# Routed rows in 256-row tiles among attention slots, and three score units for a causal group

## The chip, the cores and the metric

The kernel runs on one core of a Trainium2 chip. The metric is the device time of one execution in microseconds (us); lower is better. Five engines work side by side and meet only at semaphores: TensorE (PE; its weight loads are listed as PEld), VectorE (DVE), ScalarE (ACT), GpSimd (POOL) and SyncE (SP). In this kernel SyncE issues every DMA before the change.

## The reference, cut to what matters

```python
# x: (8, 256, 128), ctx_1024: (8, 512, 128)
x = x + tanh(g_xattn[0]) * L0_xattn(layernorm(x), ctx)      # 16 heads of 8, keys from ctx
x = x + tanh(g_ffn[0])   * L0_ffn(layernorm(x))             # one expert of eight for each row
x = x + tanh(g_xattn[1]) * L1_xattn(layernorm(x), ctx)      # self attention, cross attention, FFN, norms between
x = x + tanh(g_ffn[1])   * L1_ffn(layernorm(x))             # causal attention with rotary, then two experts of four

def L0_ffn(x):                                              # E = 8, D = 128, H = 512
    top1 = argmax(xf @ gate_w.T + gate_b)
    for e in range(8):
        y = relu(xf @ w1[e].T + b1[e]) @ w2[e].T + b2[e]
        out = out + where(top1 == e, y, 0)
```

Everything is float32. The inputs are drawn from a seed; which rows go to which expert is known only when the kernel runs.

## The kernel before

**Batches.** There are four attentions (att0: cross, att1: self, att2: cross, att3: causal) and eight batches of 256 rows in each. One number n from 0 to 31 counts them; `body(n)` is one batch of one attention. A body is a row of slots: 16 in att0 and att2 (512 keys, one head a slot), 8 in att1 and att3 (256 keys, two heads a slot). Its items are put at 16 positions, so that a slot of att1 or att3 holds two positions.

**What a slot does.** `E` multiplies keys by queries into a half of `e_ps` (1024 columns of PSUM), ScalarE takes the exponential into the ring `prob`, and `AV` multiplies by the values into `av_ps`. The softmax's row maxima are needed before `E`: the step `S` computes the same scores earlier, into one of the two halves of `s_ps` in units of 512 columns (two units for each head pair or head), and VectorE reduces each unit to maxima (`nmax`). `S` runs 2*gs + 1 slots ahead of `E`, where gs is the slots of a group of four heads. When a group is whole, GpSimd splits the maxima into bfloat16 parts (`maxsplit`), TensorE turns them (`maxT`, into `misc`), ScalarE copies them to `mrow`, and a DMA brings them into row 72 and on of `Qst`, from where the next `E` reads them.

**misc.** The PSUM buffer `misc` (512 columns) is shared by all small matmuls: projections, turns, gates. Each use first waits until the one before it was copied out (`misc_drained`).

**Order.** `all_steps()` writes one list, `STEPS`; every engine, SyncE's queue too, goes through it in this order and does its part of each step. Nothing is reordered later. Batch n's slots carry the projections of batch n + 2, the loads of n + 1 to n + 3 and the output steps of n - 1.

**First mixture.** `RUNS = [(0, B), (B, N)]` cuts the list after att0. Between the two runs `moe0_steps` does the mixture in four blocks of 512 rows. For each of eight experts and four pieces of the hidden 512, `m0.h` is a 128x512 matmul with weights `w1_0` into `e_ps` (L1496), ScalarE applies the relu into `prob` (L974), VectorE multiplies by the row's mask for that expert (L1207; the mask is spread by L1491 into `s_ps`), and `m0.down` adds the output matmul to `av_ps` (L1503). All rows go through all experts. Weights for all eight (4 MB) are loaded into `wbig` during att0. The step also writes the transposed rows that att1 loads as `inT`.

**Causal attention.** In att3 an `S` unit holds one head: two matmuls of 256 columns (L1369) and three mask matmuls of 128 (L1372, L1373, L1375), four units for a group of four heads.

## Time and profile before

| | us |
|---|---|
| median of 3 runs | 1477.69 |
| lowest, highest | 1476.61, 1484.08 |
| the profiled execution, its time | 1473.35 |
| its span, first to last instruction | 1471.6 |
| TensorE busy | 1279.9 |
| VectorE busy | 882.1 |
| ScalarE busy | 693.7 |
| GpSimd busy | 305.0 |

The mean granted clock of TensorE is 0.933 of full. All stretches below are given in us from the span's start. Matmuls are pipelined, so that a stretch in which TensorE is busy is not one in which it starts a matmul as early as it could; the distance between two starts tells that. A float32 matmul stands in the trace as two records, one for each pass.

### The profile page before, as it was taken

The numbers are of one execution on the slowest core, as the hardware profiler recorded it, in microseconds if no ns is written. First come the engines' busy times: TensorE is split into PE (matmuls) and PEld (weight loads), VectorE is DVE, ScalarE is ACT, GpSimd is POOL, SyncE is SP. The second block draws the span as 40 slices with busy tenths as digits, with TensorE's granted clock in tenths as the row PEclk, the third lists the DMA queues.
The fourth block names the chain that finished last, engine by engine and source line by source line (L and its number), as shares of the span: only waits on it lengthen the run. The fifth ranks groups of instructions, "written<-read, shape, count | busy, mean of one in ns | idle before, by whom it ended". The sixth has DMA issues, their size and how long they took to land.

```text
span 1471.6 us, 25336 instructions
## 1 busy us (share of the span) xinstructions
PE 1279.9 (87%) x8424; PEld 673.2 (46%) x8424; DVE 882.1 (60%) x1922; ACT 693.7 (47%) x1064; POOL 305.0 (21%) x896
## 2 busy tenths in 40 slices
PE   3999989979999998878879997887888788879998
PEld 1444444534444443445435444444555566634343
DVE  2777677833444444477658777868675866633333
ACT  1466566633333332566637665644533334423333
POOL 3223222100001000333422331312232322100000
PEclk9999899989999999799969999999989989869999
DMA  7554444210001300465644453533333434220110
GB/s 183 164 155 142 131 146 129 70 48 8 15 21 38 106 21 1 139 173 158 181 141 150 125 169 97 156 97 98 101 102 105 132 89 129 63 55 15 29 29 14
DMA packets 163175, 144.40 MB, mean 98 GB/s; under 512 B 11739, under 2 KB 136931, under 8 KB 163043
## 3 DMA queue, kind: packets, MB, share of 16 engines
q1 hardware_dynamic: 163046, 142.79, 33.6%
q8 instruction: 68, 1.11, 0.3%
q14 instruction: 61, 0.50, 0.1%
HBM read 79.05 MB, written 62.91 MB: 96 GB/s over the span
## 4 chain that ended last, share of the span: by engine, by line
issue 60%; POOLq 20%; PE 15%; DVE 3%; DMA 1%; DVEq 1%; ACT 1%; POOL 0%; SPq 0%; PEldq 0%; ACTq 0%
POOLq L865 4%; POOLq L838 4%; PE e_ps L1566 3%; PE av_ps L1577 3%; PE e_ps L1567 3%; POOLq L835 2%; POOLq L840 2%; POOLq L875 2%; POOLq L873 2%; POOLq L877 1%; PE misc L1558 1%; DVE nmax L1092 1%; PE s_ps L1369 1%; PE av_ps L1415 1%; PE misc L1349 1%
## 5 line engine op out<-in xcount | busy, mean ns | idle before, releaser
L924 ACT ACTIVATE prob<-e_ps 128x1024 f32<-128x1024 f32 (+1 forms) x384 | 378.1, 988 | 244.1 <-PE e_ps L1397 176.2
L1088 DVE TENSOR_REDUCE nmax<-s_ps 128x1 f32<-128x512 f32 x512 | 332.7, 686 | 115.5 <-PE s_ps L1363 113.6
L1397 PE MATMUL e_ps<-Qst,Kst 75*128 75x256 bf16 x1408 | 241.3, 285 | 19.6 <-DMA Qst<-mrow 12.6
L1363 PE MATMUL s_ps<-Kst,Qst 72*128 72x512 bf16 x512 | 206.3, 407 | 44.0 <-DVE nmax L1088 33.1
L1092 DVE TENSOR_REDUCE nmax<-s_ps 128x2 f32<-128x512 f32 x256 | 171.2, 687 | 106.2 <-PE s_ps L1369 56.4
L1415 PE MATMUL av_ps<-prob,Vx 128*32 128x256 f32 (+1 forms) x3072 | 220.6, 406 | 0.8 <-ACT OT L929 0.8
L1397 PEld LDWEIGHTS e_ps<-Qst,Kst 75*128 75x128 bf16 x1408 | 137.7, 101 | 87.6 <-issue 22.3
L1207 DVE TENSOR_TENSOR prob<-prob,s_ps 128x512 f32<-128x512 f32 x128 | 87.8, 687 | 147.4 <-ACT prob L974 146.7
L974 ACT ACTIVATE prob<-e_ps,b 128x512 f32<-128x512 f32 x128 | 87.9, 687 | 147.4 <-PE e_ps L1496 146.7
L1369 PE MATMUL s_ps<-Kst,Qst 72*128 72x256 bf16 x512 | 119.4, 294 | 22.7 <-DVE nmax L1092 21.9
L1496 PE MATMUL e_ps<-FB,wbig 128*128 128x512 f32 x256 | 137.2, 627 | 0.0
L1503 PE MATMUL av_ps<-prob,wbig 128*128 128x512 f32 x256 | 128.1, 592 | 0.0
L1415 PEld LDWEIGHTS av_ps<-prob,Vx 128*32 128x32 f32 x3072 | 92.0, 116 | 72.6 <-issue 39.7
L1363 PEld LDWEIGHTS s_ps<-Kst,Qst 72*128 72x128 bf16 x512 | 50.3, 99 | 149.3 <-DVE nmax L1088 110.4
L929 ACT ACTIVATE OT<-av_ps 128x256 f32<-128x256 f32 x128 | 49.1, 384 | 95.5 <-PE av_ps L1415 95.4
L872 POOL TENSOR_TENSOR mparts<-nmax,zeros 128x8 bf16<-128x8 f32 x128 | 25.6, 200 | 310.4 <-DVE nmax L1088 166.2
L1313 DVE TENSOR_TENSOR prob<-prob 128x512 f32<-128x512 f32 x48 | 33.2, 693 | 88.6 <-ACT prob L1012 88.1
L1503 PEld LDWEIGHTS av_ps<-prob,wbig 128*128 128x128 f32 x256 | 48.6, 190 | 61.2 <-issue 53.1
L1369 PEld LDWEIGHTS s_ps<-Kst,Qst 72*128 72x128 bf16 x512 | 48.3, 103 | 61.9 <-DVE nmax L1092 29.7
L959 ACT ACTIVATE mrow<-misc 12x256 bf16<-12x256 bf16 x128 | 46.4, 363 | 55.9 <-PE misc L1444 55.6
L1496 PEld LDWEIGHTS e_ps<-FB,wbig 128*128 128x128 f32 x256 | 47.1, 196 | 53.3 <-issue 52.3
L1011 ACT ACTIVATE prob<-e_ps 128x512 f32<-128x512 f32 x48 | 28.7, 597 | 84.4 <-PE e_ps L1567 84.3
(179 smaller groups left out, 1624.1 us busy)
## 6 DMA issues: line engine op xcount, KB each, us to landing
q_parts<-qp SPq DMA_DIRECT2D x96, 192.0 KB, 2.4
k_parts<-kp SPq DMA_DIRECT2D x48, 384.0 KB, 3.4
Qst<-q_parts SPq DMA_DIRECT2D x128, 144.0 KB
Kst<-k_parts SPq DMA_DIRECT2D x64, 288.0 KB
k_parts<-kp SPq DMA_DIRECT2D x48, 192.0 KB, 2.4
Kst<-k_parts SPq DMA_DIRECT2D x64, 144.0 KB
ctxT<-in_ctxT SPq DMA_DIRECT2D x16, 256.0 KB, 4.6
wbig<-in_w SPq DMA_DIRECT2D x16, 256.0 KB, 4.8
```

What stands on the lines that cost most here:

```text
L838: po.drain()
L924: act.activation(dst, src, ACT.Exp).then_inc(e_drained, 1)
L974: act.activation(hid[:, c % 8, :], hid_ps[:, c % 4, :], ACT.Relu, bias=b1_0[:, e, t:t + 1]) \
L1088: ve.tensor_reduce(nmax[:, g, u, h % GH:h % GH + 1], s_ps[:, u, :], AX.X, ALU.max, negate=True).then_inc(s_drained, 1)
L1092: ve.tensor_reduce(nmax[:, g, :, h % GH:h % GH + 1], s_ps[:, u, :].rearrange("p (t k) -> p t k", t=QT), AX.X, ALU.max, negate=True).then_i ...
L1207: ve.tensor_tensor(gated[:, c % 8, :], hid[:, c % 8, :], s_ps[:, mk % 2, :], ALU.mult) \
L1363: last = pe.matmul(s_ps[:, u, :], Qst[0:ROWS, par, s, u * P:u * P + P], Ks[0:ROWS, par, s, :], start=True, stop=True)
L1369: last = pe.matmul(o, Qst[0:ROWS, par, h, t * P:t * P + P], Ks[0:ROWS, par, h, 0:SQ], start=True, stop=not a.rope)
L1397: last = pe.matmul(o, Ks[0:KROWS, par, h, t * P:t * P + P], Qst[0:KROWS, par, h, :], start=True, stop=not a.rope)
L1415: last = pe.matmul(av_ps[VW * hh:VW * hh + VW, SQ - w:SQ], Vx[:, par, t, h, :], prob[:, place, off * SQ:off * SQ + w], start=(t == 0), sto ...
L1496: pe.matmul(hid_ps[:, c % 4, :], w1_0[:, e, t * P:t * P + P], x, start=True, stop=True) \
L1503: pe.matmul(av_ps[:, :], w2_0[:, e, t, :], gated[:, c % 8, :], start=False, stop=end) \
```

## The change

It does three things.

**Rows by expert.** Eight batches make two halves (`HALF` = 4). As each batch of att0 ends, its rows are normed into `zg`, gated (`m0.gate`), the expert is chosen (`m0.choose`), and `m0.rank` counts by matmul how many earlier rows of the half chose the same expert. When the half is complete, `m0.plan` makes two tables: `ypos`, the place of each row in a list sorted by expert, where each expert starts at a multiple of 256, and `widx`, the weight rows of each of the NT = 11 tiles. GpSimd then issues indexed DMAs: `m0.scatter` writes rows of `zg` to their places in `xs_rows` (zeroed at the start from `blank`), `m0.wload` reads a tile's weights and biases (128 rows of 1032 numbers) into a ring of four. For each tile follow `m0.xT` (turn), `m0.h` (4 matmuls of 256 columns), `m0.down` (4 more), `m0.back` (turn) and a store to `ys_rows`.

**Among the slots.** `RUNS` is one run. `moe0_items` puts the steps at positions: for the first half tiles in bodies 5 and 6, for the second in 9 and 10, a tile every 4/3 positions. att1's batches no longer load `inT`. They load `x1`, gather their rows of `ys_rows` by `ypos` (GpSimd), add (`xstat`), norm (`xapply`), turn (`xT`) and store x2 and z (`xstore`).

**Causal groups.** In att3 a group of four heads is three `S` units: one with the first 128 rows of all four heads against the first 128 keys, two with the other 128 rows of two heads each. The third mask is gone.

```diff
-RUNS = [(0, B), (B, N)]
+RUNS = [(0, N)]
...
+def moe0_items():
+    it = {}
+    def put(n, p, *steps):
+        it.setdefault((n + p // 16, p % 16), []).extend(steps)
+    for b in range(B):
+        if b % HALF < HALF - 1:
+            for p, kind in ((3, "m0.gate"), (6, "m0.choose"), (9, "m0.rank")):
+                put(b + 2, p, (kind, b, None))
+    for g in range(B // HALF):
+        last = HALF * g + HALF - 1
+        n = last + 1
+        for p, kind in ((12, "m0.gate"), (13, "m0.choose"), (14, "m0.rank")):
+            put(n, p, (kind, last, None))
+        for k in range(3):
+            put(n, 15 + k, ("m0.plan", g, k))
+        n += 1
+        put(n, 0, ("m0.wload", g, 0), ("m0.wload", g, 1))
+        for j in range(GT):
+            put(n, 2 + j // 4, ("m0.scatter", g, j))
+        put(n, 4, ("m0.wload", g, 2), ("m0.wload", g, 3), ("m0.xload", g, 0), ("m0.xload", g, 1))
+        for k in range(NT):
+            p = 5 + 4 * k // 3
+            put(n, p, ("m0.xT", g, k))
+            if k + 2 < NT:
+                put(n, p, ("m0.xload", g, k + 2))
+            put(n, p + 1, ("m0.h", g, k))
+            put(n, p + 2, ("m0.down", g, k))
+            if k + WRING < NT:
+                put(n, p + 2, ("m0.wload", g, k + WRING))
+            put(n, p + 3, ("m0.back", g, k))
+        m = B + HALF * g
+        put(m - 2, 9, ("loadx", m, None))
+        put(m - 2, 11, ("xstat", m, None), ("loadx", m + 1, None))
+        put(m - 2, 13, ("xapply", m, None), ("xT", m, None))
+        put(m - 2, 14, ("q", m, None), ("qsplit", m, None), ("xstore", m, None))
+        put(m - 2, 15, ("k", m, None), ("ksplit", m, 0), ("xstat", m + 1, None))
+        put(m - 1, 0, ("qstore", m, None))
+        put(m - 1, 2, ("kstore", m, None))
+    return it
...
-    if n + 2 < hi:
-        if n + 2 < B:
+    if n + 2 < hi and not opens_half(n + 2):
+        if n + 2 < 2 * B:
             put(0, ("xapply", n + 2, None))
             put(1, ("xT", n + 2, None))
+            if n + 2 >= B:
+                put(2, ("xstore", n + 2, None))
...
-def moe0_steps(plan):
...
+                elif kind == "m0.xload":
+                    if arg == 0:
+                        sp.wait_ge(m0_sent, 16 * GT * (n + 1))
+                    if m0_tile(n, arg):
+                        prev = (n, arg - 2) if arg >= 2 else (n - 1, NT - 1 if (NT - 1) % 2 == arg else NT - 2)
+                        sp.wait_ge(misc_filled, MISC[("m0.xT",) + prev] + 1)
+                    src = xs_rows[n][arg * TILE:(arg + 1) * TILE, :].rearrange("(t p) d -> p t d", p=P)
+                    sp.dma_start(xs_in[:, arg % 2, :, :], src).then_inc(m0_xin[arg % 2], 16)
+                elif kind == "m0.back":
+                    sp.wait_ge(misc_drained, MISC[(kind, n, arg)] + 1)
+                    dst = ys_rows[n][arg * TILE:(arg + 1) * TILE, :].rearrange("(t p) d -> p t d", p=P)
...
+                elif kind == "xstore":
+                    sp.wait_ge(x_normed, n + 1)
+                    sp.dma_start(batch_rows("x2", b), xr[:, par, :, :]).then_inc(x_stored[par], 16)
+                    sp.dma_start(batch_rows("z", b), xn[:, :, :]).then_inc(z_stored, 16)
...
+            for g in range(B // HALF):
+                blank = dram["blank"].unsqueeze(0).to_broadcast([NT, TILE, D])
+                sp.dma_start(xs_rows[g].rearrange("(n r) d -> n r d", r=TILE), blank).then_inc(blank_stored, 16)
...
+                elif kind == "m0.wload":
                     po.drain()
-                    po.wait_ge(f_stats, f_stat("m0", n, 0))
-                    rsqrt(LF, BT, False).then_inc(f_rstd, 1)
+                    po.wait_ge(m0_planned, 2 * n + 1)
+                    if arg >= WRING:
+                        po.wait_ge(misc_drained, MISC[("m0.down", n, arg - WRING)] + 1)
+                    elif n:
+                        po.wait_ge(misc_drained, MISC[("m0.down", n - 1, NT - 1)] + 1)
+                    index = bass.IndirectOffsetOnAxis(ap=widx[:, n, arg:arg + 1], axis=0)
+                    po.indirect_dma_start(out=w_0[:, arg % WRING, :], out_offset=None, in_=dram["w_0"], in_offset=index) \
+                        .then_inc(m0_win[arg % WRING], 16)
+                elif kind == "m0.scatter":
+                    po.drain()
+                    po.wait_ge(m0_planned, 2 * n + 2)
+                    po.wait_ge(blank_stored, 16 * B // HALF)
+                    index = bass.IndirectOffsetOnAxis(ap=ypos[:, n, arg:arg + 1], axis=0)
+                    po.indirect_dma_start(out=xs_rows[n], out_offset=index, in_=zg[:, arg, :], in_offset=None) \
+                        .then_inc(m0_sent, 16)
+                elif kind == "loadx" and n >= B:
+                    par, g = n % 2, (n - B) // HALF
+                    po.drain()
+                    po.wait_ge(m0_ystored[0], 16 * Y_EVEN * (g + 1))
+                    po.wait_ge(m0_ystored[1], 16 * Y_ODD * (g + 1))
+                    po.wait_ge(x_stats, n - 1)
+                    for t in range(QT):
+                        j = QT * (n % HALF) + t
+                        index = bass.IndirectOffsetOnAxis(ap=ypos[:, g, j:j + 1], axis=0)
+                        po.indirect_dma_start(out=yg[:, par, t, :], out_offset=None, in_=ys_rows[g], in_offset=index) \
+                            .then_inc(y_back[par], 16)
                 elif kind == "f.stat":
...
+                elif kind == "m0.xT":
+                    act.wait_ge(misc_filled, MISC[st] + 1)
+                    if arg >= 2:
+                        act.wait_ge(e_filled, SLOT[("m0.h", n, arg - 2)] + 1)
+                    act.activation(xs_T[:, arg % 2, :], misc[:, 0:TILE], ACT.Copy).then_inc(misc_drained, 1)
                 elif kind == "m0.h":
...
+                    for t in range(H0 // P):
+                        b1 = w_0[:, arg % WRING, 2 * H0 + t:2 * H0 + t + 1]
+                        last = act.activation(m0_hid[:, arg % 2, t * TILE:(t + 1) * TILE],
+                                              e_ps[:, c % 2, t * TILE:(t + 1) * TILE], ACT.Relu, bias=b1)
...
+                    elif a.rope:
+                        k = s % a.gs * a.units(0) + u
+                        dst = nmax[:, g, 1, 2 * k - 2:2 * k] if k else nmax[:, g, 0, :]
+                        ve.tensor_reduce(dst, s_ps[:, c % 2, :].rearrange("p (h k) -> p h k", h=2 if k else GH), AX.X,
+                                         ALU.max, negate=True).then_inc(s_drained, 1)
...
                 elif kind == "xstat":
                     ve.wait_ge(x_loaded[par], 16 * (n // 2 + 1))
+                    if n >= B:
+                        ve.wait_ge(y_back[par], 16 * QT * ((n - B) // 2 + 1))
+                        ve.scalar_tensor_tensor(out=xr[:, par, :, :], in0=yg[:, par, :, :], scalar=gate_of("moe0"),
+                                                in1=xr[:, par, :, :], op0=ALU.mult, op1=ALU.add)
...
-                        apply_norm(LA, dst, newres[:, par, :, :], QT).then_inc(norm_ready, 1)
+                        if n >= HALF:
+                            ve.wait_ge(m0_sent, 16 * GT * (n // HALF))
+                        j = QT * (n % HALF)
+                        apply_norm(LA, zg[:, j:j + QT, :], newres[:, par, :, :], QT).then_inc(norm_ready, 1)
                     else:
...
+                    elif a.rope:
+                        g, k = s // a.gs, s % a.gs * a.units(0) + u
+                        heads, t, w = (range(2 * k - 2, 2 * k), 1, SQ) if k else (range(GH), 0, P)
+                        for x, h in enumerate(heads):
+                            o = s_ps[:, c % 2, x * w:x * w + w]
+                            h += GH * g
+                            pe.matmul(o, Qst[0:ROWS, par, h, t * P:t * P + P], Ks[0:ROWS, par, h, 0:w], start=True,
+                                      stop=False)
+                            last = pe.matmul(o[:, w - P:w], identb[:, :], maskb[:, 0, :], start=False, stop=True)
...
+                elif kind == "m0.rank":
+                    if n == 0:
+                        pe.wait_ge(below_made, 1)
                     pe.wait_ge(m0_chosen, n + 1)
-                    for t in range(BT):
-                        last = pe.transpose(misc[0:E0, :].bitcast(BF16)[:, t * P:t * P + P], ohb[:, t, :], identb[:, :])
+                    total = misc[:, QT * E0:QT * E0 + E0]
+                    pe.matmul(misc[:, 0:E0], below[:, :], ohb[:, 0, :], start=True, stop=True)
+                    pe.matmul(misc[:, E0:2 * E0], below[:, :], ohb[:, 1, :], start=True, stop=False)
+                    pe.matmul(misc[:, E0:2 * E0], onesb[:, :], ohb[:, 0, :], start=False, stop=True)
+                    pe.matmul(total, onesb[:, :], ohb[:, 0, :], start=True, stop=False)
+                    pe.matmul(total, onesb[:, :], ohb[:, 1, :], start=False, stop=True).then_inc(misc_filled, 1)
+                elif kind == "m0.xT":
+                    pe.wait_ge(m0_xin[arg % 2], 16 * (m0_tile(n, arg) + 1))
+                    turn(misc, lambda t: xs_in[:, arg % 2, t, :], QT).then_inc(misc_filled, 1)
+                elif kind == "m0.h":
+                    c = SLOT[st]
+                    pe.wait_ge(m0_win[arg % WRING], 16 * (w_uses(n, arg) + 1))
+                    pe.wait_ge(misc_drained, MISC[("m0.xT", n, arg)] + 1)
+                    pe.wait_ge(e_drained, c - 1)
+                    for t in range(H0 // P):
+                        last = pe.matmul(e_ps[:, c % 2, t * TILE:(t + 1) * TILE], w_0[:, arg % WRING, t * P:t * P + P],
+                                         xs_T[:, arg % 2, :], start=True, stop=True)
+                    last.then_inc(e_filled, 1)
+                elif kind == "m0.down":
+                    pe.wait_ge(e_drained, SLOT[("m0.h", n, arg)] + 1)
+                    for t in range(H0 // P):
+                        w2 = w_0[:, arg % WRING, H0 + t * P:H0 + t * P + P]
+                        last = pe.matmul(misc[:, 0:TILE], w2, m0_hid[:, arg % 2, t * TILE:(t + 1) * TILE],
+                                         start=t == 0, stop=t == H0 // P - 1)
                     last.then_inc(misc_filled, 1)
-                elif kind == "m0.mask0":
-                    pe.wait_ge(misc_drained, MISC[("m0.spread", n, None)] + 1)
```

On TensorE, in body 5. In the names `FB` with `ident` is a turn of a tile (`m0.xT` or `m0.back`), `FB` with `wbig` is `m0.h`, `m_hid` with `wbig` is `m0.down`. Before, from the values of batch 6 on:

```order
L1438 MATMUL misc<-wts,ctxT 128x128 x4
L1363 MATMUL s_ps<-Kst,Qst 128x512
L1397 MATMUL e_ps<-Qst,Kst 128x256 x4
L1363 MATMUL s_ps<-Kst,Qst 128x512
L1455 MATMUL misc<-wts,aT 128x128 x2
L1415 MATMUL av_ps<-prob,Vx 32x256 x8
```

and the same place after:

```order
L1560 MATMUL misc<-wts,ctxT 128x128 x4
L1470 MATMUL misc<-ident,FB 128x128 x2
L1613 MATMUL e_ps<-FB,wbig 128x256 x4
L1470 MATMUL misc<-ident,FB 128x128 x2
L1484 MATMUL s_ps<-Kst,Qst 128x512
L1521 MATMUL e_ps<-Qst,Kst 128x256 x4
L1484 MATMUL s_ps<-Kst,Qst 128x512
L1577 MATMUL misc<-wts,aT 128x128 x2
L1620 MATMUL misc<-m_hid,wbig 128x256 x4
L1613 MATMUL e_ps<-FB,wbig 128x256 x4
L1470 MATMUL misc<-ident,FB 128x128 x2
L1537 MATMUL av_ps<-prob,Vx 32x256 x8
```

In one slot seven groups for the tiles now stand where none stood, four of them on `misc`.

On GpSimd, in body 5. Before:

```order
L837 TENSOR_TENSOR qk<-qk,qp 128x256
L839 CAST qp<-qk 128x256
L841 TENSOR_TENSOR qp<-qk,qp 128x256
L872 TENSOR_TENSOR mparts<-nmax,zeros 128x2x4
L874 TENSOR_TENSOR mres<-nmax,mparts 128x8
```

and after (`wbig<-in_w,widx` is `m0.wload`, `xs_rows<-wbig,ypos` is `m0.scatter`):

```order
L941 DMA wbig<-in_w,widx 128x1032 x2
L883 TENSOR_TENSOR qk<-qk,qp 128x256
L885 CAST qp<-qk 128x256
L887 TENSOR_TENSOR qp<-qk,qp 128x256
L948 DMA xs_rows<-wbig,ypos 2816x128 x4
L918 TENSOR_TENSOR mparts<-nmax,zeros 128x2x4
L920 TENSOR_TENSOR mres<-nmax,mparts 128x8
L922 CAST mparts<-mres 128x2x4
L924 TENSOR_TENSOR mparts<-mres,mparts 128x2x4
L948 DMA xs_rows<-wbig,ypos 2816x128 x4
```

Ten indexed DMAs now stand around the first `maxsplit` of the body.

On SyncE, at the start of the program, after the change:

```order
L703 DMA gw<-in_gw 128x4
L868 DMA xs_rows<-in_blank 11x2x16384 x2
L806 DMA q_parts<-qp 128x3x256 x3
L811 DMA k_parts<-kp 128x3x512 x3
L821 DMA Qst<-q_parts 72x1024
```

The two copies of zeros stand between the last constant and the first batch's Q.

## Rows read from the trace of the kernel before

**Rows 1.** The page: busy us, share of the span, instructions of each engine.
```profile
PE 1279.9 (87%) x8424; PEld 673.2 (46%) x8424; DVE 882.1 (60%) x1922; ACT 693.7 (47%) x1064; POOL 305.0 (21%) x896
```

**Rows 2.** Stages: length; busy us of PE, PEld, DVE, ACT, POOL; PE clock; DMA share; GB/s.
```profile
48.00:303.00 255.00, 232.00 (x1980) 124.66 (x1979) 188.83 (x384) 164.98 (x230) 66.67 (x200) 0.96 0.45 129
303.00:594.80 291.80, 272.03 (x746) 118.55 (x745) 119.11 (x242) 100.51 (x154) 14.45 (x31) 0.94 0.12 35
594.80:773.50 178.70, 150.07 (x1210) 83.33 (x1209) 117.40 (x245) 103.00 (x167) 62.83 (x196) 0.86 0.53 157
1073.00:1295.00 222.00, 187.24 (x1918) 134.75 (x1915) 150.92 (x399) 84.22 (x151) 63.56 (x198) 0.89 0.35 103
```

**Rows 3.** Exp alone (L924): length, ACT busy (count) by stretch; then two starts.
```profile
47.00:303.00 256.00, 128.39 (x126) 0.96 0.45 130
...
301.46 3.00 ACT L924 ACTIVATE prob<-e_ps 128x1024 f32<-128x1024 f32 x3
...
594.76 1.02 ACT L924 ACTIVATE prob<-e_ps 128x1024 f32<-128x1024 f32 x1 [4.21 <-PE e_ps L1397]
```

**Rows 4.** Groups, 303:594.8, PE: shapes, count | busy us, mean ns | idle before, releasers.
```profile
L1369 PE MATMUL s_ps<-Kst,Qst 72*128 72x256 bf16 x22 | 5.3, 347 | 4.8 <-DVE nmax L1092 4.5 <-PE av_ps L1503 0.3
L1349 PE MATMUL misc<-ident,OT 128*128 128x128 f32 x24 | 4.8, 336 | 1.1 <-DVE att_o L1139 0.7 <-DVE lg L1188 0.4
...
L1415 PE MATMUL av_ps<-prob,Vx 128*32 128x256 f32 x48 | 3.0, 382 | 0.8 <-ACT OT L929 0.8
L1349 PE MATMUL misc<-ident,FB 128*128 128x128 f32 x16 | 2.4, 272 | 0.0
L1430 PE MATMUL misc<-inT,wts 128*128 128x256 f32 x8 | 2.4, 379 | 0.0
L1397 PE MATMUL e_ps<-Qst,Kst 75*128 75x256 bf16 x12 | 2.3, 321 | 3.6 <-DMA Qst<-mrow 3.6
...
L1455 PE MATMUL misc<-wts,aT 128*128 128x128 f32 x4 | 1.2, 460 | 0.5 <-ACT aT L963 0.5
```

**Rows 5.** Timeline, PE, inside the mixture: start, us, line, operation, count.
```profile
571.46 1.02 PE L1496 MATMUL e_ps<-FB,wbig 128*128 128x512 f32 x2
572.32 1.02 PE L1503 MATMUL av_ps<-prob,wbig 128*128 128x512 f32 x2
```

**Rows 6.** Timeline, PE, ahead of the mixture, with [idle before <-releaser].
```profile
313.62 1.12 PE L1349 MATMUL misc<-ident,OT 128*128 128x128 f32 x4 [0.72 <-DVE att_o L1139]
...
316.62 1.22 PE L1455 MATMUL misc<-wts,aT 128*128 128x128 f32 x4 [0.47 <-ACT aT L963]
```

**Rows 7.** Waits (us in total, times, longest), 48:303; then those of PE, 594:773.
```profile
PEld s_ps L1363 <- DVE nmax L1088: 38.0, 72, 1.9
...
PE e_ps L1397 <- DMA Qst<-mrow: 11.5, 11, 3.6
```

**Rows 8.** Groups, ACT, whole span: copy of 256 columns with a bias.
```profile
L938 ACT ACTIVATE qk<-misc,qbias 128x256 f32<-128x256 f32 x24 | 11.3, 470 | 8.5 <-PE misc L1430 8.5
```

**Rows 9.** Timeline of SyncE's queue at the start; then a stretch as in rows 2.
```profile
6.91 5.39 SPq L658 DMA_DIRECT2D ropes<-in_ropes  x1
...
18.89 1.47 SPq L767 DMA_DIRECT2D q_parts<-qp  x3
...
29.68 0.31 SPq L785 DMA_DIRECT2D Kst<-k_parts  x1
...
25.00:50.00 25.00, 16.52 (x36) 3.98 (x36) 13.03 (x24) 3.85 (x7) 7.67 (x19) 1.00 0.68 197
```

**Rows 10.** Timeline, PE and DVE, one S unit of the fourth attention.
```profile
1181.42 0.27 PE L1369 MATMUL s_ps<-Kst,Qst 72*128 72x256 bf16 x1
1181.53 0.22 PE L1372 MATMUL s_ps<-maskb,identb 128*128 128x128 bf16 x1
1181.59 0.22 PE L1373 MATMUL s_ps<-maskb,identb 128*128 128x128 bf16 x1
...
1182.01 0.69 DVE L1092 TENSOR_REDUCE nmax<-s_ps 128x2 f32<-128x512 f32 x1
```

535 lines of the change are left out of this document (250 added, 285 removed).

## The prediction

> **What bounds the kernel now.** I read the page's totals first, then the busy times by stage, then in each stage which wait ends last.
>
> TensorE is busy for 87% of the span and VectorE for 60% [rows 1]; the others come behind. By stage [rows 2] TensorE is at 91% in the first attention, at 93% between 303 and 594.8 us, where the first mixture lies, at 84% in the second attention and in the fourth. The mixture is TensorE alone: half the way through one hidden and one output matmul of 512 columns leave in 0.86 us each, two passes of 0.43 us, with no gap [rows 5], and all four blocks pay for all eight experts. The last Exp of the eighth batch starts at 303.4 (the third of three from 301.46), the first of the ninth at 594.76 [rows 3]: 291.4 us without a score. That is a fifth of the span, and the change aims at it.
>
> The attention stages are not bound by TensorE's columns. A slot of the first attention takes 256/126 = 2.03 us [rows 3], and the waits there are for the row maxima that VectorE takes, 38.0 us of them [rows 7]. In the second attention TensorE also waits for the maxima's way through GpSimd and DMA, 11.5 us for the DMA that brings them to `Qst` [rows 7].
>
> **The change part by part.** The sum is made against the profiled span.
>
> *The dense mixture goes.* Of the 291.4 us, attention work stays and only moves: in the window's groups [rows 4] S 5.3, OT turns 1.6 (8 of the 24; 4.8/3), AV 3.0, projections 2.4, E 2.3, and five more kinds, the largest of them the projection by the output weights with 1.2, for which I count 3.7 in all. That is 18.3 us, so **−273**.
>
> *Twenty-two tiles come.* Four batches are 1024 rows; tiles of 256 rows with eight experts make 4 + 7 = 11 in a run, and there are two runs. A tile has 8 matmuls of 256 columns in float32. A pass of 512 columns is 0.43 us, two passes a matmul, so 256 columns cost 0.43: 3.4 us. Four turns of 128 columns are 0.15 each (2.4 us for 16 [rows 4]), 0.6. Five groups each end in a pipeline that the next cannot overlap; I give 0.1 us to each: 4.5 us of TensorE. Besides, a tile uses the one PSUM buffer `misc` three times, and each use waits until the last one was drained. Such a round trip is 0.72 us over VectorE and 0.47 over ScalarE in the row before the mixture [rows 6]. The order puts `m0.back`, `m0.down`, `m0.h`, `m0.xT` side by side, so I count two of the three as unhidden: 1.2. ScalarE has six copies of 256 columns in a tile, at most 0.47 us each [rows 8], 2.8 us against 5.7: it keeps up. The hidden units lie behind about one slot of attention before `m0.down` wants them, so I take this as hidden. 5.7 us a tile, **+125**. Ends: 4.5 (all round trips covered; slots of 2.03 us hold room for that) and 8.5 (ScalarE's 2.8 us stands in the path of each tile), so +99 to +187.
>
> *Routing per batch.* Gate and rank are seven small matmuls with two uses of `misc`, 0.72 + 0.47 us of round trips [rows 6], and a dozen short VectorE operations in front of the maxima, which delay TensorE by their length at most. The gate work of before was inside the stage taken away. I take 2 us a batch between 1 (the round trips alone) and 3.5: **+16** (8 to 28).
>
> *Opening of a run.* GpSimd now issues two weight gathers and eight scatters before the first `m0.xload`, and SyncE waits there for all scatters. Behind it in SyncE's queue stand the max rows of the running batch and its Q and K. No row shows an indexed DMA. The nearest rows are SyncE's issues, from 0.31 us for a K load to 5.39 for the rope tables [rows 9]. I take 1.0 us, nearer the short end, since the long one stood at a full queue. Ten issues are 10 us, where the batch has four positions: 8 us in the first attention, 5 in the second, and then three slots until the max rows are wanted. I take 3 + 9 = **+12** (3 to 40).
>
> *Start.* Two copies of 1.44 MB of zeros stand in SyncE's queue ahead of the first Q and K stores. At full share the queues there move 197/0.68 = 290 GB/s [rows 9]: 10 us from about 18.9, with Q and K (1.8 MB, 6 us) behind it, where K is wanted at 29.68. 18.9 + 10 + 6 = 34.9, **+5** (0 to 14). On this the Trainium skill says more: by its page "DMA: Bandwidth & Descriptors", section "Why a DMA increments its semaphore by 16 and not by 1", a copy is spread on the largest number of engines up to 16 that divides its slowest dimension, here 11 tiles, hence 11 engines. By that the zeros would take 14.5 us and the term would be +9.5. No row here shows such a copy; it stays inside the bounds.
>
> *Second attention.* It no longer loads its input but makes it: statistics, norm and turn for each batch, with two gathers on GpSimd, 2.0 us by the price above, in a stage where GpSimd stands between maxima and E [rows 7], and one more `misc` round trip of 0.47. 8 batches at 2.5 us, **+20** (8, nearly all hidden, to 40, issues of 2 us and more), and at the two places where a half opens the gather has two positions to land, **+5** (2 to 10). The loads and stores of the old block form go; they were off the path.
>
> *Fourth attention.* Three S units per group for four. A unit of before leaves in 0.40 us (two of 256 columns at 0.11, three masks at 0.06) and its maximum takes 0.69 [rows 10]. A group now has 0.48 + 2×0.34 = 1.16 us for 1.6, and one maximum less. Over 32 groups that is 14 us of TensorE and 22 of VectorE. At 84% TensorE and with both engines relieved I take **−16** (−5 to −22).
>
> Sum: −273 + 125 + 16 + 12 + 5 + 20 + 5 − 16 = −106. 1471.6 − 106 = 1365.6 us of span. The profiled run took 1473.35, and the median of the three is 1477.69, 6.1 above the span: **1372 us**.
>
> One rule of the Trainium skill speaks against the change. "SBUF — State Buffer", section "Who interferes with whom", says that a DMA issued by GpSimd cannot have its descriptors written while VectorE runs a copy, cast or tensor_scalar in its two-port mode. Rows show such VectorE work only as short pairs of norm instructions beside long maxima, so by it each issue might wait some tenths of a microsecond, 10 us in all for 54 issues; no trace here has such a DMA yet.
>
> **The rivals.**
> *Round trips hidden.* The slots' own room (2.03 us against a TensorE content near 1.7) and VectorE's freed time cover them: tiles at 4.5 us, openings 5, routing 10, second attention 12. −273 + 99 + 10 + 5 + 5 + 12 + 3 − 18 = −157: 1321. For it: waits for maxima fall away where tiles stretch a slot. Against: each misc use has one buffer.
> *Latency in the path.* Tiles at 8.5 us because ScalarE's relus sit between h, down and the next misc drain, as the queue order allows: 22 × 2.8 = +62, 1434. For it: `m0.xT` is drained behind the relus of `m0.h`.
> *Slower.* Indexed DMAs are dear on GpSimd. Each extra microsecond per issue costs 20 us at the openings (ten issues, twice) and some 10 at the 16 gathers in the second attention, which are partly covered: 30 in all; the 22 weight gathers stay behind four tiles of lead. From 1.0 + 106/30 = 4.5 us per issue the gain is gone; at 5 us the kernel takes 1493. For it: the 5.39 us row. Against: that one waited for a full queue.
> *Not doing what it says.* The tiles come, but serialised behind SyncE's waits so that attention does not run beside them. Then the work adds as in the sum, since TensorE is the bound either way; it falls in with the second rival.
>
> **How the numbers follow.** Forecast, a gain of 75 to 135 us: 0.63. Hidden round trips: 0.19. Latency in the path or issues near 3 us: 0.12. Issues of 4.5 us or more: 0.05 (0.01 of it no change). No change by other mishaps: 0.01. The range for 8 in 10 is 1318 to 1434: it cuts half of the hidden case, and beyond the latency case. About 0.5% is what a measurement of this kernel can tell from no change: faster by more 0.94, within 0.02, slower 0.04.
>
> **What would show it.** Weight matmuls of 256 columns 0.43 us apart; about 6 us of TensorE time per tile, and idle time before `misc` matmuls ended by ScalarE and VectorE; at both openings a hole before an E, ended by the max rows' DMA, near 3 and 9 us; the first Exp about 5 us later than before; bodies 13 to 15 a little longer than now; the fourth attention at about 206 us for 222. A weight gather that ends idle time of TensorE would make the tile term wrong; a GpSimd issue above 3 us would make the opening wrong.

## The result, and the profile after

The changed kernel takes 1490.87 us (median; 1480.98 to 1501.68), the kernel before, timed beside it, 1474.61 us. The ratio is 1.013, with a 95% interval of 1.010 to 1.016. The forecast was 1372 us. A gain of 7% was expected and a loss of 1.3% came.

The profiled execution took 1501.18 us, with a span of 1499.4; that is 10 us above its own median, where the profiled execution of before lay near its own. The traces therefore differ by more (27.8 us of span) than the medians (16.3). The page's totals, in the columns of [rows 1]:

```profile
PE 1161.3 (77%) x8192; PEld 658.8 (44%) x8192; DVE 797.7 (53%) x1863; ACT 654.2 (44%) x1069; POOL 363.1 (24%) x958
```

TensorE has 119 us less to do than in [rows 1], and the kernel is not faster: it waits. The waits of TensorE from 230 to 600 us, a stretch that holds both openings (us in total, times, longest):

```profile
PE misc L1470 <- DMA FB<-xs_rows: 43.1, 2, 29.0
PE misc L1566 <- POOL mparts L924: 23.1, 3, 15.1
```

Stretches cut at the bodies' first Exps, in the columns of [rows 2]: length; busy us of PE, PEld, DVE, ACT, POOL; clock; DMA share; GB/s. The second and the fourth hold the tiles of the two halves.

```profile
55.00:242.00 187.00, 162.62 (x1299) 86.59 (x1297) 133.69 (x307) 108.60 (x154) 50.88 (x144) 0.94 0.39 118
242.00:425.00 183.00, 124.31 (x754) 77.37 (x753) 62.31 (x143) 67.70 (x128) 39.27 (x75) 0.82 0.28 87
...
493.50:657.40 163.90, 95.12 (x538) 66.51 (x536) 39.81 (x99) 51.54 (x110) 37.15 (x71) 0.78 0.29 88
657.40:801.40 144.00, 106.54 (x775) 58.44 (x776) 82.25 (x181) 67.53 (x109) 49.73 (x139) 0.79 0.49 148
801.40:1108.00 306.60, 263.27 (x2122) 140.92 (x2120) 222.60 (x487) 172.62 (x242) 80.97 (x228) 0.94 0.41 122
```

In the two stretches with tiles TensorE is busy for 68% and 58%, where it was at 93% in the dense mixture [rows 2].

Two starts of the Exp, as in [rows 3]. The first comes 6.9 us later than before (47.94 then):

```profile
54.87 1.02 ACT L994 ACTIVATE prob<-e_ps 128x1024 f32<-128x1024 f32 x1 [5.80 <-PE e_ps L1521]
```

```profile
801.39 1.94 ACT L994 ACTIVATE prob<-e_ps 128x1024 f32<-128x1024 f32 x2 [0.38 <-PE e_ps L1521]
```

Now the first opening on GpSimd, part of body 5 (start, us, line, operation, idle before). L941 is a weight gather, L948 a scatter, L918 to L924 the split of a group of maxima:

```profile
245.99 1.18 POOL L941 DMA_INDIRECT wbig<-in_w,widx  x1 [3.67 <-DVE widx L1327]
252.18 0.95 POOL L941 DMA_INDIRECT wbig<-in_w,widx  x1 [5.01 <-issue]
256.41 0.67 POOL L883 TENSOR_TENSOR qk<-qk,qp 128x256 f32<-128x256 f32 x1 [3.28 <-issue]
...
259.32 1.03 POOL L948 DMA_INDIRECT xs_rows<-wbig,ypos  x1 [0.88 <-issue]
262.49 0.99 POOL L948 DMA_INDIRECT xs_rows<-wbig,ypos  x1 [2.13 <-issue]
265.59 0.97 POOL L948 DMA_INDIRECT xs_rows<-wbig,ypos  x1 [2.11 <-issue]
...
282.46 0.96 POOL L948 DMA_INDIRECT xs_rows<-wbig,ypos  x1 [2.10 <-issue]
```

The DMA itself is recorded with 1.0 us, the price that the forecast took. But the next instruction comes 3.1 us after a scatter's start and 6.2 and 4.2 us after a weight gather's. Between them stands `po.drain()`. How long a scatter takes from its issue to its landing, in us, from the DMA issues between 259 and 284 us:

```profile
xs_rows<-wbig,ypos POOLq DMA_INDIRECT x8, 2.2
```

The drains stand in the trace as records of their own. Those ahead of the scatters, with their shortest, median and longest time in ns:

```profile
L944 POOLq DRAIN  x16: 301/2537/2607, 257.7 to 531.2; - x16
```

In the whole trace 46 drains stand behind an indexed DMA that had not landed when they began. They last 2.5 to 6.8 us, and every one of them ends 0.07 to 0.13 us after the last of these DMAs has landed, whether that takes 2.2 us from the issue (a scatter) or 6.5 (the slowest weight gather). The other 902 drains last 0.29 us in the median and 1.10 at most, as the 894 in the kernel before do. So the length of such a drain is the landing of the DMA, and from its end to the start of the next scatter pass another 0.8 us.

SyncE's queue at the same time. It stands at `m0.xload` (L715) until all scatters have landed, and the maxima's row (L828) is behind it:

```profile
247.90 0.36 SPq L824 DMA_DIRECT2D Kst<-k_parts  x1
284.70 0.89 SPq L715 DMA_DIRECT2D FB<-xs_rows  x2
285.64 0.73 SPq L828 DMA_DIRECT2D Qst<-mrow  x1
```

And TensorE, which waits first for the split of the maxima and then for the first tile's rows:

```profile
257.05 0.38 PE L1484 MATMUL s_ps<-Kst,Qst 72*128 72x512 bf16 x1
272.52 0.37 PE L1566 MATMUL misc<-identb,mparts 128*12 128x128 bf16 x2 [15.09 <-POOL mparts L924]
286.92 0.66 PE L1470 MATMUL misc<-ident,FB 128*128 128x128 f32 x2 [14.02 <-DMA FB<-xs_rows]
```

In the second half, in att1, the two holes are 7.8 and 29.0 us.

**Where the 134 us between forecast and trace lie.** The first Exps of the 32 bodies cut the span. Each term of the sum against what the cuts show, in us of span; the last column is an experiment's kernel, below.

| term | forecast | changed kernel | self_wait |
|---|---|---|---|
| dense mixture goes (body 7 with the mixture: 312.4, then 35.6 and 34.2) | -273 | -277 | -278 |
| 22 tiles | +125 | +143 | +132 |
| openings, both halves | +12 | +74 | +33 |
| routing, second attention, landing (16 + 20 + 5) | +41 | +81 | +62 |
| start | +5 | +7 | -2 |
| third attention | 0 | +7 | +10 |
| fourth attention and what follows | -16 | -7 | -10 |
| sum | -106 | +28 | -53 |

The tile row is made from the slots with tile steps: 101.6 us in the bodies 5 and 6 where the same slots took 28.3 before, and 86.8 for 17.3 in the bodies 9 and 10. An opening is the slots from a body's start to its first tile: body 5's slots 0 to 5 took 48.9 us for 13.9, body 9's slots 0 to 2 took 47.1 for 8.1.

The drains, which self_wait takes out, and the zeros, which it moves, account for some 80 of the 134 us (a span of 1419.1 for 1499.4). The other 53 are still there in its column, 21 of them at the openings and 21 in the row of routing and second attention.

### The profile page after: what moved, and what is told of

It reads as the page before. It is cut to its first block, busy times and chain, and to the rows that moved or that the text cites. A ratio compares the mean times of both kernels' runs of the same rounds, so it can differ in the third digit from the quotient of the medians.

```text
span 1499.4 us, 25002 instructions
## 1 busy us (share of the span) xinstructions
PE 1161.3 (77%) x8192; PEld 658.8 (44%) x8192; DVE 797.7 (53%) x1863; ACT 654.2 (44%) x1069; POOL 363.1 (24%) x958
## 4 chain that ended last, share of the span: by engine, by line
issue 54%; POOLq 22%; PE 17%; DVE 2%; ACT 2%; DMA 1%; POOL 1%; DVEq 1%; SPq 0%; ACTq 0%; PEldq 0%
POOLq L911 5%; POOLq L884 4%; PE e_ps L1678 3%; PE av_ps L1689 3%; PE e_ps L1679 3%; PE misc L1620 2%; POOLq L881 2%; POOLq L886 2%; PE e_ps L1613 2%; POOLq L919 2%; POOLq L921 2%; POOLq L923 2%; PE misc L1470 1%; POOLq L944 1%; PE misc L1670 1%
## 5 line engine op out<-in xcount | busy, mean ns | idle before, releaser
L1537 PE MATMUL av_ps<-prob,Vx 128*32 128x256 f32 (+1 forms) x3072 | 234.2, 427 | 0.0
L1176 DVE TENSOR_REDUCE nmax<-s_ps 128x2 f32<-128x512 f32 x128 | 86.4, 687 | 164.8 <-PE s_ps L1498 164.3
L1484 PEld LDWEIGHTS s_ps<-Kst,Qst 72*128 72x128 bf16 x512 | 51.4, 101 | 148.4 <-DVE nmax L1167 99.4
L918 POOL TENSOR_TENSOR mparts<-nmax,zeros 128x8 bf16<-128x8 f32 x128 | 26.3, 205 | 357.5 <-DVE nmax L1167 198.9
L1172 DVE TENSOR_REDUCE nmax<-s_ps 128x2 f32<-128x512 f32 (+1 forms) x96 | 65.9, 687 | 57.7 <-PE s_ps L1494 57.3
L1566 PE MATMUL misc<-identb,mparts 128*12 128x128 bf16 x256 | 37.6, 232 | 63.7 <-POOL mparts L924 35.6
L1470 PE MATMUL misc<-ident,FB 128*128 128x128 f32 x136 | 27.3, 298 | 75.1 <-DMA FB<-xs_rows 43.1
L1620 PE MATMUL misc<-m_hid,wbig 128*128 128x256 f32 x176 | 54.2, 461 | 14.8 <-DVE FB L1343 10.4
L1498 PE MATMUL s_ps<-Kst,Qst 72*128 72x256 bf16 x256 | 54.4, 308 | 4.0 <-DVE nmax L1176 3.3
L1470 PEld LDWEIGHTS misc<-ident,FB 128*128 128x128 f32 x136 | 16.5, 149 | 88.8 <-issue 47.4
L883 POOL TENSOR_TENSOR qk<-qk,qp 128x256 f32<-128x256 f32 x32 | 21.5, 671 | 133.0 <-ACT qp L1007 101.9
```

What stands on the lines that cost most here:

```text
L1172: ve.tensor_reduce(dst, s_ps[:, c % 2, :].rearrange("p (h k) -> p h k", h=2 if k else GH), AX.X, ALU.max, negate=True).then_inc(s_drained, 1)
L1176: ve.tensor_reduce(nmax[:, g, :, h % GH:h % GH + 1], s_ps[:, c % 2, :].rearrange("p (t k) -> p t k", t=QT), AX.X, ALU.max, negate=True).th ...
L1470: last = pe.transpose(dst[:, t * P:t * P + P], src(t), ident[:, :])
L1484: last = pe.matmul(s_ps[:, c % 2, :], Qst[0:ROWS, par, s, u * P:u * P + P], Ks[0:ROWS, par, s, :], start=True, stop=True)
L1498: last = pe.matmul(s_ps[:, c % 2, t * SQ:t * SQ + SQ], Qst[0:ROWS, par, h, t * P:t * P + P], Ks[0:ROWS, par, h, 0:SQ], start=True, stop=True)
L1537: last = pe.matmul(av_ps[VW * hh:VW * hh + VW, SQ - w:SQ], Vx[:, par, t, h, :], prob[:, place, off * SQ:off * SQ + w], start=(t == 0), sto ...
```

## The experiments

All ratios are of times against the kernel before, timed beside each kernel; the changed kernel's own is 1.013.

**Leaving out the scatters** (no_scatter). SyncE waits for the plan instead.

```diff
-                elif kind == "m0.scatter":
-                    po.drain()
...
-                        .then_inc(m0_sent, 16)
...
                     if arg == 0:
-                        sp.wait_ge(m0_sent, 16 * GT * (n + 1))
+                        sp.wait_ge(m0_planned, 2 * n + 2)
+                        sp.wait_ge(blank_stored, 16 * B // HALF)
```

> The changed kernel without the 16 scatters: the rows are not written to their places, so the tiles run on rows of zeros and the result of the first mixture is left out; everything else stays. SyncE waits for the plan and the zeros in place of the scatters. Theory A (an indexed DMA holds GpSimd for 3.1 us where it writes rows and for 4 to 6 us where it loads weights, and SyncE and the row maxima stand behind that): 16 x 3.1 = 50 us of GpSimd go from the two openings, where TensorE idles 15.1 + 14.0 and 7.8 + 29.0 us; 1430 to 1445 us for 1491. Theory B (the time is lost in the tiles themselves, by latency and a low clock): 1475 to 1490.

Measured: 1436.92 us, ratio 0.970 (0.965 to 0.976), 54 us less by the medians and 63 by the ratios, so 3.4 to 3.9 us for each scatter. No wait for `FB<-xs_rows` is left, and in the traces the two openings took 38 us for 96. Theory A holds, Theory B falls. The loss against the kernel before lies at the openings.

**No drain ahead of an indexed DMA** (no_drain).

```diff
                 elif kind == "m0.wload":
-                    po.drain()
                     po.wait_ge(m0_planned, 2 * n + 1)
...
                 elif kind == "m0.scatter":
-                    po.drain()
...
                     par, g = n % 2, (n - B) // HALF
-                    po.drain()
```

> The changed kernel without the drain of GpSimd ahead of each indexed DMA (three places in the code). Theory A1 (the drain waits until the DMA before it is through, an issue by itself is short): scatters follow each other in 1.3 us as the two gathers of one batch do, 16 x 1.8 = 29 us go from the openings and some more at the weight loads; 1440 to 1460 us for 1491. Theory A2 (GpSimd works that long on each indexed DMA, and the drain only shows it): the distance stays near 3 us and the time at 1485 to 1491.

Measured: 1457.49 us, ratio 0.987 (0.981 to 0.993). Taking out three lines makes the change a gain of 1.3%. GpSimd in the same opening:

```profile
243.29 1.18 POOL L940 DMA_INDIRECT wbig<-in_w,widx  x1 [3.68 <-DVE widx L1324]
244.78 0.95 POOL L940 DMA_INDIRECT wbig<-in_w,widx  x1 [0.30 <-issue]
252.43 0.67 POOL L883 TENSOR_TENSOR qk<-qk,qp 128x256 f32<-128x256 f32 x1 [6.70 <-issue]
...
257.22 0.96 POOL L946 DMA_INDIRECT xs_rows<-wbig,ypos  x1 [0.30 <-issue]
258.49 0.97 POOL L946 DMA_INDIRECT xs_rows<-wbig,ypos  x1 [0.30 <-issue]
261.09 0.19 POOL L918 TENSOR_TENSOR mparts<-nmax,zeros 128x8 bf16<-128x8 f32 x1 [1.63 <-issue]
```

Scatters now follow each other in 1.27 us, not 3.1: A1. But the idle time has only moved to the next drain, the one at the head of a split: 6.70 us behind two weight gathers, 1.63 behind four scatters. A drain on GpSimd waits until the indexed DMAs before it have landed: in this trace the second weight gather lands 7.42 us after its issue at 244.78, at 252.20, and the split behind it starts at 252.43.

**The opening's steps spread over more positions** (spread), drains as they are.

```diff
-        put(n, 0, ("m0.wload", g, 0), ("m0.wload", g, 1))
-        for j in range(GT):
-            put(n, 2 + j // 4, ("m0.scatter", g, j))
-        put(n, 4, ("m0.wload", g, 2), ("m0.wload", g, 3), ("m0.xload", g, 0), ("m0.xload", g, 1))
+        for k, p in enumerate((3, 5, 7, 8)):
+            put(n, p, ("m0.wload", g, k))
+        for j, p in enumerate((2, 2, 3, 4, 4, 5, 6, 6)):
+            put(n, p, ("m0.scatter", g, j))
+        put(n, 7, ("m0.xload", g, 0), ("m0.xload", g, 1))
         for k in range(NT):
-            p = 5 + 4 * k // 3
+            p = 8 + 4 * k // 3
```

> The changed kernel with the tiles of each half three positions later and the indexed DMAs of the opening set one or two to a position (scatters at positions 2 to 6, weight gathers at 3, 5, 7, 8, the first loads of rows at 7), drains as in the changed kernel. Theory A: three more positions of attention (2.0 us each in the first half, 1.2 in the second) cover GpSimd's work before SyncE stands at the scatters, and a group of maxima waits for fewer DMAs; 1465 to 1480 us for 1491. Theory B: 1488 to 1495, since the tiles and their pace are the same.

Measured: 1496.14 us, ratio 1.012 (1.005 to 1.020), the same as the changed kernel. A's number (1465 to 1480) was wrong here, B's (1488 to 1495) was right within a microsecond. TensorE's waits:

```profile
PE misc L1471 <- DMA FB<-xs_rows: 65.4, 2, 36.7
...
PE misc L1567 <- POOL mparts L925: 4.8, 2, 4.3
```

43.1 + 23.1 = 66 us of waits became 65.4 + 4.8 = 70, and the bodies 5, 6, 9 and 10 took 351 us for 347. My reading, which no run tests by itself: GpSimd's work is the chain, and where it is laid decides only which wait sees it, since three positions of attention also bring GpSimd more splits, and the tiles stand at the end of the same queue.

**Zeros later** (late_blank). The two copies go behind an E in the middle of the second and third batch.

```diff
-            for g in range(B // HALF):
-                blank = dram["blank"].unsqueeze(0).to_broadcast([NT, TILE, D])
-                sp.dma_start(xs_rows[g].rearrange("(n r) d -> n r d", r=TILE), blank).then_inc(blank_stored, 16)
-            for st in STEPS[4:]:
+            for i, st in enumerate(STEPS[4:]):
+                if st[0] == "E" and st[2] == 8 and st[1] in (1, 2):
+                    blank = dram["blank"].unsqueeze(0).to_broadcast([NT, TILE, D])
+                    sp.dma_start(xs_rows[st[1] - 1].rearrange("(n r) d -> n r d", r=TILE), blank) \
+                        .then_inc(blank_stored, 16)
                 step(*st)
```

> The changed kernel with the two copies of zeros taken from the start and put in the middle of the second and of the third batch. If the zeros stand ahead of the first Q and K, the first Exp comes 5 to 7 us earlier (54.9 to about 48 us) and the time is 1484 to 1486 for 1491. If something else moved the start (routing constants, weights in another order), it stays at 1491 and the first Exp at 54.9.

Measured: 1485.81 us, ratio 1.009 (1.006 to 1.012). The first Exp is back where it was, so the zeros were the whole of the start term:

```profile
47.76 1.02 ACT L995 ACTIVATE prob<-e_ps 128x1024 f32<-128x1024 f32 x1 [5.80 <-PE e_ps L1522]
```

**Leaving out the gathers of the second attention** (no_gather).

```diff
-                elif kind == "loadx" and n >= B:
...
-                            .then_inc(y_back[par], 16)
...
-                        ve.wait_ge(y_back[par], 16 * QT * ((n - B) // 2 + 1))
-                        ve.scalar_tensor_tensor(out=xr[:, par, :, :], in0=yg[:, par, :, :], scalar=gate_of("moe0"),
+                        ve.scalar_tensor_tensor(out=xr[:, par, :, :], in0=xr[:, par, :, :], scalar=gate_of("moe0"),
```

> The changed kernel without the 16 gathers of the mixture's rows in the second attention (drains elsewhere as in the changed kernel). The result of the first mixture is left out: the new rows are the old rows plus themselves by the gate, in an instruction of the same shape. Against the changed kernel's 1491. Theory A (the gathers and the drains behind them stand in GpSimd's queue ahead of the row maxima): the holes of 9.6 us before the first batch's turn, 5.2 and 5.4 us before turns of maxima go, and the tails of the batches 6 and 10 shorten; 1455 to 1468 us. Theory B (the second attention got longer by its own statistics, norms and stores): 1480 to 1490.

Measured: 1478.01 us, ratio 1.000 (0.998 to 1.003), 13 us less by the medians and 19 by the ratios for 16 gathers. It lies between the two theories, nearer to B: about a microsecond each, and most of the 81 us in the row of routing and second attention is not the gathers.

**GpSimd waits for its own instructions, not for a drain** (self_wait). This contains no_drain and late_blank, and replaces each drain in GpSimd's arithmetic:

```diff
+            def done(inst, sem=po_done):
+                signals[id(sem)] = signals.get(id(sem), 0) + 1
+                last_op[:] = [(sem, signals[id(sem)])]
+                return inst.then_inc(sem, 1)
+
+            def fence():
+                if last_op:
+                    po.wait_ge(*last_op[0])
...
-                po.drain()
+                fence()
...
-                po.tensor_tensor(r[:, c0:c1], src[:, c0:c1], parts[:, 0, c0:c1], ALU.subtract)
-                po.drain()
-                po.tensor_copy(parts[:, 1, c0:c1], r[:, c0:c1])
-                po.drain()
+                done(po.tensor_tensor(r[:, c0:c1], src[:, c0:c1], parts[:, 0, c0:c1], ALU.subtract))
+                fence()
+                done(po.tensor_copy(parts[:, 1, c0:c1], r[:, c0:c1]))
+                fence()
```

> Three edits together on the changed kernel: no drain ahead of an indexed DMA, the zeros in the middle of the second and third batch, and in all of GpSimd's arithmetic (splits of Q, K and the maxima, the roots of the norms) each drain replaced by a semaphore that the instruction before it sets, so that nothing on GpSimd waits for a DMA that it issued. Theory A (what holds GpSimd is the drain until the DMA is through): the two weight gathers of an opening hold it for 1.3 us each, no longer 9.3 us together, the openings shrink by some 8 us each and the holes of 5 us in the second attention go; with the 5 us of the start 1425 to 1440 us. Theory B (GpSimd's own work on a DMA sets the pace): 1448 to 1455, the start alone.

Measured: 1423.97 us, ratio 0.966 (0.960 to 0.972), faster than both kernels. Theory A again, 1 us below its range. The change is now worth 3.4%, half of the 7% that was forecast. GpSimd goes from a scatter straight into a split and back:

```profile
237.35 0.97 POOL L962 DMA_INDIRECT xs_rows<-wbig,ypos  x1 [0.31 <-issue]
238.63 0.96 POOL L962 DMA_INDIRECT xs_rows<-wbig,ypos  x1 [0.30 <-issue]
239.61 0.22 POOL L934 TENSOR_TENSOR mparts<-nmax,zeros 128x8 bf16<-128x8 f32 x1
...
244.96 0.96 POOL L962 DMA_INDIRECT xs_rows<-wbig,ypos  x1 [0.30 <-issue]
245.95 0.67 POOL L897 TENSOR_TENSOR qk<-qk,kp 128x256 f32<-128x256 f32 x1
```

**The same edit on the kernel before** (before_self_wait), which has no DMA on GpSimd, tells whether drains cost this by themselves.

```diff
-                po.drain()
+                fence()
```

> The kernel before with the drains in GpSimd's arithmetic replaced by semaphores as in self_wait, and nothing else. It has no DMA on GpSimd. Theory A (in self_wait the edit pays because a drain there waits for DMAs): a split of maxima gets some 0.1 us shorter here, 1465 to 1476 for 1475. Theory H (drains cost that much by themselves, wherever they stand): some 25 us less, 1445 to 1455.

Measured: 1480.39 us beside 1480.0, ratio 0.997 (0.992 to 1.002): no difference. Theory H falls. So the 2% that self_wait has over no_drain, less the half per cent of the zeros, come from drains that stood behind indexed DMAs.

**Each scatter twice** (scatters_twice), on self_wait.

```diff
-                    po.indirect_dma_start(out=xs_rows[n], out_offset=index, in_=zg[:, arg, :], in_offset=None) \
-                        .then_inc(m0_sent, 16)
+                    for rows in (xs_rows, xs_twin):
+                        po.indirect_dma_start(out=rows[n], out_offset=index, in_=zg[:, arg, :], in_offset=None) \
+                            .then_inc(m0_sent, 16)
```

> The kernel of self_wait with every scatter issued twice, the second to rows that nobody reads: 16 more indexed DMAs of the same size ahead of the first tiles. Theory A (without a drain behind it an indexed DMA holds GpSimd 1.28 us): 16 x 1.28 = 20 us more, 1444 us (1440 to 1448). If the price were 3.1 us also without a drain, 50 us more, 1474; if GpSimd has room there, 1424 to 1430.

Measured: 1452.6 us, ratio 0.982 (0.975 to 0.989), 24 to 29 us above self_wait where Theory A had 20: 1.5 to 1.8 us for each. That is a little above the 1.28 us of the issue, far below 3.1. The price of an issue without a drain is near what the forecast took.

**TensorE kept busy in the hole** (warm_fill), on no_drain: 48 matmuls that nobody reads ahead of the first tile's turn.

```diff
+                    if arg == 0:
+                        for _ in range(48):
+                            pe.matmul(misc[:, 0:SQ], identb[:, :], maskb[:, :, :].rearrange("p a b -> p (a b)"), start=True,
+                                      stop=True)
                     pe.wait_ge(m0_xin[arg % 2], 16 * (m0_tile(n, arg) + 1))
```

> The changed kernel without the drains ahead of indexed DMAs (1457 us) and with 48 matmuls of 256 columns in bfloat16, whose result nobody reads, ahead of the turn of the first tile of each half, where TensorE idles 8.3 and 15.3 us. Theory C (a good part of the loss is TensorE's clock, which is granted at 0.50 in the holes and for some 8 us behind them): with TensorE busy in the hole the clock stands at 1.00 behind it, a matmul of the first tiles takes half as long, 3 to 5 us less at each opening, 1448 to 1453 us. Theory A alone: 1457, or up to 10 us more where the filling outlasts the hole.

Measured: 1455.55 us, ratio 0.987 (0.982 to 0.992), the same as no_drain. The clock did what Theory C says. First no_drain, then warm_fill, behind the hole; the line with `Vx` is 16 records of AV:

```profile
271.14 0.66 PE L1467 MATMUL misc<-ident,FB 128*128 128x128 f32 x2 [8.32 <-DMA FB<-xs_rows]
271.73 1.94 PE L1534 MATMUL av_ps<-prob,Vx 128*32 128x256 f32 x16
```

```profile
259.98 6.99 PE L1604 MATMUL misc<-maskb,identb 128*128 128x256 bf16 x48 [0.47 <-ACT mrow L1024]
267.66 0.44 PE L1467 MATMUL misc<-ident,FB 128*128 128x128 f32 x2 [0.69 <-DMA FB<-xs_rows]
268.03 1.07 PE L1534 MATMUL av_ps<-prob,Vx 128*32 128x256 f32 x16
```

The same 16 records take 1.07 us, not 1.94, and still the time stays within what can be told apart. The intervals alone, some 8 us on either side, could hide Theory C's gain. The traces say more: the bodies 5, 6, 9 and 10, which hold the openings and the tiles, took 306 us in both. The low clock in and behind a hole (granted 0.50, which is 1.2 GHz, in no_drain from 263 to 273 us) is a companion of the loss and not a part of it that this filling could buy back; the filling itself ran at 0.77 in the mean, from 260 to 267 us.

**The causal groups alone** (att3_alone), on the kernel before: the part of the change on att3 as it stands in the diff ahead of the prediction, without the rest.

```diff
+    def units(self, s):
+        return 1 if self.rope and s % self.gs else 2
```

> The kernel before, with nothing but the causal groups of three S units (that part of the change alone). The prediction's term was -16 us (-5 to -22); the changed kernel shows the fourth attention 8 us shorter. Theory D (the term was mis-sized: TensorE is not the bound there, the maxima's way and the mixture's steps are): 1464 to 1470 us for 1476. Theory E (-16 holds by itself and something of the rest of the change gives 8 back): 1458 to 1462.

Measured: 1466.98 us, ratio 0.991 (0.988 to 0.995), 10 to 13 us less for a forecast of 16. Theory D's number holds.

**Tiles closer together and later** (tiles_later), and with the first batch's rows asked for earlier (tiles_later_early_x); the latter edit alone (early_x). All three on self_wait.

```diff
+        for k, p in enumerate((5, 6, 7, 8)):
+            put(n, p, ("m0.wload", g, k))
+        for j, p in enumerate((2, 2, 3, 3, 4, 4, 5, 5)):
+            put(n, p, ("m0.scatter", g, j))
+        put(n, 6, ("m0.xload", g, 0), ("m0.xload", g, 1))
...
-            p = 5 + 4 * k // 3
+            p = 8 + k
...
-        put(m - 2, 9, ("loadx", m, None))
+        put(m - 2, 6, ("loadx", m, None))
```

> The kernel of self_wait (1424 us) with each half's tiles three positions later and then one to every position in place of one to 4/3, so that the last one ends where it did; the scatters two to a position from 2 to 5, weight gathers behind them at 5, 6, 7, 8, the first loads of rows at 6. Theory A: the holes ahead of the first tile's turn (8.4 and 12.7 us) are covered by three positions of attention, 6 us of the first and 4 of the second; the tiles, which TensorE and the round trips bound, cost the same when they are closer; 1410 to 1418 us. Theory B (tiles closer together wait for each other: one every position leaves less attention between two uses of misc): no gain, 1422 to 1432.

> tiles_later and besides the x and y rows of the first batch of each half of the second attention asked for at position 6, right behind the last tile, not at 9. In self_wait GpSimd issues that gather 8.3 us after the last store of a tile, and TensorE idles 9.2 us before the batch's turn. Theory A (the place in the order holds the gather, not its landing): 3 to 6 us less than tiles_later, 1405 to 1414. Theory B (the norm behind it, which keeps its positions, is as late as before): the same as tiles_later.

> The kernel of self_wait with the x and y rows of the first batch of each half asked for at position 6 and not at 9, the tiles where they are. From tiles_later_early_x against tiles_later (5.5 us less): 1417 to 1421 us. If the gain there came only from tiles that end later, 1424.

Measured: 1425.26, 1419.71 and 1425.38 us; ratios 0.967, 0.961 and 0.963, with 0.006, 0.005 and 0.010 on either side. None can be told from self_wait's 0.966, so the gains that Theory A had in the first two expectations did not come; for tiles_later and for early_x the number without a gain (1422 to 1432; 1424) is the one that held, and tiles_later_early_x lies between its two. TensorE's waits, tiles_later and then early_x:

```profile
PE misc L1484 <- DMA FB<-xs_rows: 21.4, 2, 14.2
PE misc L1484 <- DVE xn L1136: 15.5, 4, 9.2
```

```profile
PE misc L1483 <- DMA FB<-xs_rows: 21.1, 2, 12.7
...
PE misc L1483 <- DVE xn L1135: 11.4, 5, 4.5
```

The holes before the tiles stayed at 21 us, as in self_wait, although the tiles begin three positions later: with splits of Q, K and maxima between them the eight scatters took 14.5 us from the first start to the end of the last, where they took 11.2 in self_wait. The bodies 5, 6, 9 and 10 together took 296 us for self_wait's 299. The late gather's hole went from 9.2 to 4.5 us and the time did not follow, so something behind it was as late; what it was stays open.

**A quarter of the columns** (tiles_quarter), on self_wait.

```diff
-                        last = pe.matmul(e_ps[:, c % 2, t * TILE:(t + 1) * TILE], w_0[:, arg % WRING, t * P:t * P + P],
-                                         xs_T[:, arg % 2, :], start=True, stop=True)
+                        last = pe.matmul(e_ps[:, c % 2, t * TILE:t * TILE + 64], w_0[:, arg % WRING, t * P:t * P + P],
+                                         xs_T[:, arg % 2, 0:64], start=True, stop=True)
...
-                        last = pe.matmul(misc[:, 0:TILE], w2, m0_hid[:, arg % 2, t * TILE:(t + 1) * TILE],
+                        last = pe.matmul(misc[:, 0:64], w2, m0_hid[:, arg % 2, t * TILE:t * TILE + 64],
```

> The kernel of self_wait with 64 columns in place of 256 in the 8 matmuls of each tile; three quarters of each tile's two products are left out, with ScalarE's copies and all waits at their size. 8 x 0.43 us shrink to a quarter, 2.6 us a tile, 57 us for 22. Theory F (the tile's price is TensorE's columns, as in the sum): 1424 - 57 = 1367 us, down to 1375. Theory G (round trips over misc and ScalarE's copies set the pace of a tile): at most half of it, 1395 to 1415.

Measured: 1415.66 us, ratio 0.962 (0.956 to 0.968), for 1367 expected by F. Theory F falls as a rule for the time. But the two are not told apart by it, because the granted clock was another. The tiles of the first half, self_wait and then tiles_quarter:

```profile
251.00:361.00 110.00, 87.97 (x546) 59.20 (x539) 37.35 (x78) 48.26 (x98) 14.65 (x33) 0.94 0.35 105
```

```profile
251.00:361.00 110.00, 91.50 (x538) 60.70 (x538) 35.20 (x75) 47.24 (x96) 15.29 (x34) 0.68 0.37 109
```

With 2.6 us a tile less to do, TensorE was granted 0.68 in place of 0.94 and was busy for as long as before; the slots with tile steps took 96 us in both. In the tiles of the second half the clock was 0.68 for 0.96 as well, and these slots took 74.8 us for 81.7: 7 us of the 57 came.

**Shorter copies, all matmuls** (short_copies), on self_wait: the round trips made shorter and TensorE's work left alone.

```diff
+                        w = TILE if m0_tile(n, arg) < 1 else 64
                         last = act.activation(m0_hid[:, arg % 2, t * TILE:t * TILE + w],
                                               e_ps[:, c % 2, t * TILE:t * TILE + w], ACT.Relu, bias=b1)
...
+                    w = TILE if m0_tile(n, arg) < 1 else 64
+                    act.activation(ys_T[:, arg % 2, 0:w], misc[:, 0:w], ACT.Identity, bias=b2).then_inc(misc_drained, 1)
```

> The kernel of self_wait (1424 us) with the tiles' copies out of PSUM cut from 256 to 64 columns from the third tile on (turned rows, hidden units, output, and VectorE's copy of the turned output), all matmuls at full width; three quarters of each tile's values are stale, the result of the first mixture is left out. ScalarE has six such copies of 0.40 to 0.47 us in a tile, VectorE one of 0.42. Theory G (round trips over misc set the pace): each gets some 0.15 us shorter, three in the path of a tile and the relus, 0.5 to 1 us a tile, 1402 to 1414 us. Theory F (TensorE's columns set it, and tiles_quarter got its 57 us back by a clock of 0.68 for 0.94): 1420 to 1425, at the same clock.

Measured: 1412.04 us, ratio 0.956 (0.947 to 0.964); the medians' 12 us are Theory G's number, though the intervals touch. In the traces the slots with tile steps took 90.9 + 74.8 us for self_wait's 96.2 + 81.7: 12.2 us less, 0.6 for each of the 20 shortened tiles, at about the same clock:

```profile
251.00:361.00 110.00, 93.24 (x574) 63.28 (x567) 37.53 (x85) 41.50 (x99) 14.37 (x33) 0.92 0.37 112
```

The copies that were shortened, ScalarE in that stretch, mean ns; the first row is a relu, of which a tile has four:

```profile
L1069 ACT ACTIVATE m_hid<-e_ps,wbig 128x64 f32<-128x64 f32 x36 | 8.3, 314 | 13.8 <-PE e_ps L1630 13.8
L1069 ACT ACTIVATE m_hid<-e_ps,wbig 128x256 f32<-128x256 f32 x8 | 3.1, 474 | 2.6 <-PE e_ps L1630 2.6
```

0.16 us less for each of six ScalarE copies gave 0.6 us a tile. By the sum, with two of three round trips open and the relus hidden, it would have been 0.3. So the copies are in the path of a tile, and more of them than the sum had, as far as 12 us can be told from none.

## Why the prediction was wrong, point by point

**The dense mixture's price was right**: -277 for -273.

**The tiles were nearly right**: 6.5 us each in the changed kernel, 6.0 in self_wait, for 5.7. The columns cost what the sum took: eight records, four matmuls of 256 columns, start 1.83 us before the next group.

```profile
326.93 1.99 PE L1620 MATMUL misc<-m_hid,wbig 128*128 128x256 f32 x8 [0.61 <-DVE tmp L1245]
328.76 1.89 PE L1613 MATMUL e_ps<-FB,wbig 128*128 128x256 f32 x8
```

The total was right and its working only in part: it added columns and round trips as if each could be bought back by itself. tiles_quarter shows that columns gave back 7 us of 57 here, with the clock at 0.68, and short_copies that round trips gave back twice what the sum had open. The sign of a wrong tile term, a weight gather that ends idle time of TensorE, did not show.

**The opening of a run is the step that failed**: +12 forecast, +74 measured. The text priced "1.0 us" for an indexed DMA from SyncE's issues, and the record of the DMA does last 1.0 us. What it left out is the wait for the landing. It stood in the text's own diff as a `po.drain()` ahead of each weight gather and scatter; the kernel has one more at the head of each split behind them. With the drain an issue costs 3.1 us for a scatter and 4.2 to 6.2 for a weight gather. The path was another too: the text looked for holes of 3 and 9 us ahead of an E, ended by the DMA of the maxima. They stand ahead of two uses of `misc`, ended by the split of the maxima (15.1 and 7.8 us) and by the first tile's rows (14.0 and 29.0). Its own sign, "a GpSimd issue above 3 us would make the opening wrong", is what came.

In the kernel before, the chain that ended last already had a fifth of the span in GpSimd's queue (POOLq), most of it at lines of drains, and the text did not read that row of its page:

```profile
issue 60%; POOLq 20%; PE 15%; DVE 3%; DMA 1%; DVEq 1%; ACT 1%; POOL 0%; SPq 0%; PEldq 0%; ACTq 0%
```

The row shows where drains stand, not what they cost: before_self_wait took them out of that kernel and gained nothing.

The Trainium skill had the missing number: by "DMA: Bandwidth & Descriptors", section "Anatomy of one DMA — SWDGE (gpsimd) path", such a DMA takes about 2.0 us fixed, most of it until the last byte is confirmed, plus its bytes by 436 GB/s. For a scatter's 64 KB that is 2.15 us as an estimate, and the trace has 2.2. For a weight gather's 528 KB it is 3.2 us, and the trace has 3.9 to 6.5, so there the measurement decides. The page does not say that a drain waits for it.

**The rival "slower"** had dear issues on GpSimd, with its turning point at 4.5 us per issue and 1493 us for 5 (1492 by its own 30 us for each microsecond). The ten issues of the first opening took from 245.99 to 282.46 + 3.1 us, less some 4 us of splits, so 3.6 us each. By the rival's own rate that is 2.6 x 30 = 78 us, 1450; the time came out at 1491 because other terms were off in the same direction. So its number came near by luck. Issues near 3 us had a share in the 0.12 of another line. The rival's chance of 0.05 rested on the fullness of SyncE's queue, the wrong resource.

**Routing, second attention and landing**: +81 for 41, and still +62 without drains. The bodies 2 to 4 took 17 us more (6 in self_wait), body 8, with the gate, rank and plan of the second half, 13; the rest of the bodies 6 and 10, where the first batch's input is made, 10 and 15; the bodies 11 to 15, 26 (16 in self_wait). The term of 2.5 us for a batch of att1 was mis-sized. The likely reason, not shown, is that in slots of 2.5 us a round trip, statistics, a norm and a turn have no cover. no_gather shows that the gathers are 13 to 19 us of it. What each of the other steps costs was not measured apart.

**The start** was right: +5 for 7 and its cause too. Beside it the text had put what the Trainium skill says ("DMA: Bandwidth & Descriptors", section "Why a DMA increments its semaphore by 16 and not by 1"), eleven engines for such a copy. The trace agrees: the two copies are 44 packets of 64 KB, and eleven at a time start, near 19.1, 21.8, 24.3 and 26.7 us, the last ending at 31.4. But three of the four rounds took 2.4 to 2.9 us, some 290 GB/s from eleven engines (an estimate from 11 x 64 KB in 2.45 us), as much as the sum had given to all. So the zeros took 12.3 us, for 10 in the sum and 14.5 by the text's estimate.

**The two-port rule** of the Trainium skill that spoke against the change ("SBUF — State Buffer", section "Who interferes with whom") is hardly tested here. In the changed kernel no VectorE work lies beside a scatter, and beside the weight gathers only reductions, two-input operations and statistics, which are not among the instructions that the text named. Six of the 16 row gathers of the second attention do have a norm's tensor_scalar beside them: they are recorded with 0.95 to 1.16 us where the other ten have 0.95 to 1.04, and land after 2.6 to 3.8 us where all have 2.5 to 4.2. A wait of some tenths for each issue does not show.

**The fourth attention**: -7 in the changed kernel, 10 to 13 us less alone, for 16; inside its range, and mis-sized by a fifth to a third by itself. That it gives less beside the rest of the change was not traced further.

**The third attention** got 7 us longer with an unchanged order, for which the sum had 0. It lies in the bodies 19 (6.3 us) and 21 (3.6), in 19 at the hidden units of the FFN (`f.h`). The stretch in body 19, before and after:

```profile
874.00:885.00 11.00, 9.36 (x67) 4.79 (x68) 4.70 (x10) 5.33 (x8) 4.25 (x10) 1.00 0.47 127
```

```profile
904.00:915.00 11.00, 10.60 (x52) 4.83 (x56) 3.24 (x6) 2.29 (x3) 2.14 (x5) 0.71 0.35 104
```

The stage is longer in all traces of the changed kernel and its variants (by 3 to 14 us), but before_self_wait has 3.5 of it too. Why the clock falls there stays open.

Together: openings 62, routing and second attention 40, tiles 18, fourth attention 9, third 7, start 2, dense -4: the 134 us.

## What to carry to other kernels

Price an indexed DMA on GpSimd by what is queued behind it: the issue is about 1.3 us, but a drain behind it waits for the landing, and a queue that was written with drains before GpSimd issued DMAs is worth rewriting with semaphores that name the instruction waited for (1457 to 1424 us here, some 5 of them by moving the zeros). When a routed form replaces a dense one, cost the work that makes the lists and moves the rows as a chain (plan, scatter, load, first tile) and not as a sum of small items, since the order of every queue makes the engines wait for its end. Moving steps of such a chain to other positions brought nothing here; making the chain shorter did.

## What the runs showed of the hardware that was not expected

- A drain on GpSimd waits for the landing of the indexed DMAs before it: 46 drains end 0.07 to 0.13 us after it, and all others last 1.10 us at most. Between scatters GpSimd idles 2.11 us with it and 0.30 without, and 6.70 us behind two weight gathers. Replacing the drains in its arithmetic by semaphores gave about 1.7% where GpSimd issues DMAs (0.987 to 0.966, less the zeros' 0.4%), and nothing where it does not (0.997, 0.992 to 1.002).
- Taking 2.6 us of columns from each tile left TensorE's busy time the same in the first half's tiles, at a granted clock of 0.68 for 0.94. Filling a hole with 48 matmuls brought full speed behind it (1.07 us for 1.94 on the same 16 records) without a shorter kernel.
- The copies of zeros, with 11 tiles as their slowest dimension, ran as eleven packets of 64 KB at a time, and these moved some 290 GB/s (an estimate from 11 x 64 KB in 2.45 us).
